# Attention and feed-forward layer: rewritten instruction orders at the opening, step 4, the change of phase and the end

## The chip, the cores and the metric

The kernel runs on one core of a Trainium2 chip. The metric is the device time of one execution in microseconds. Engines: PE (TensorE), DVE (VectorE), ACT (ScalarE), POOL (GpSimd) and SP (SyncE), which here only issues DMAs. They run side by side and meet at semaphores.

## The reference

x has 8 x 1024 x 512 elements, float32. Two blocks, each with a residual and a layernorm:

```python
q = (x @ Wq.T + bq).reshape(B, S, H, D)      # k, v likewise; q, k = rope(q), rope(k); H 16, D 32
qk = einsum('bshd,bstd->bsht', q, k) / sqrt(D)
att = softmax(qk, axis=-1)                   # over the 16 heads of one position
out = einsum('bsht,bstd->bshd', att, v)
out = swapaxes(out, 1, 2).reshape(B, S, E)
x = layernorm(x + out @ Wo.T + bo)
g = einsum('th,ih->ti', x, gate_w) * gate_s  # gate, up, down: ternary, 1408 wide
u = einsum('th,ih->ti', x, up_w) * up_s
x = layernorm(x + einsum('ti,hi->th', silu(g) * u, down_w) * down_s)
```

## The kernel before

**Precision.** Operands are split into a high and a low part, and a product takes hi x hi, hi x lo and lo x hi: `project` (L594 to L604) runs 12 matmuls of 128 x 512 for one tile and one weight.

**Phase 1, attention.** 64 tiles of 128 rows make 32 units (UNITS) of two tiles, t = 0 and 1. A unit m runs through a pipeline over five steps: split_x and low_x (high and low part of x), project_qk and project_v (PE), add_bias, sines (DVE), rotate (POOL, two instructions: cosine and add), turn_k and turn_q (DVE transposes), spread_k (ACT, four copies), score (PE, 128 small matmuls), subtract_top (DVE), exponent (ACT), sums_of_prob, scale_prob, turn_prob (DVE), spread_p (ACT, four copies), weigh_values (PE, 128 small matmuls, which needs v8, loaded again from DRAM by load_v after store_v), high_of_heads (ACT), low_of_heads (DVE), project_heads (PE, the output projection, row t of each unit), add_residual, aggregate (DVE), rstd_of (POOL), shift_of (DVE), normalise_x1 (ACT), turn_x1 (DVE), store_x1. Step s does unit s - 1's projections and score, unit s - 2's softmax and weigh_values, unit s - 3's heads and unit s - 4's layernorm. Every engine has its own written order. Steps 0 to 3 are written out for each engine (on SP and, before, for step 3 on DVE, through `step`), step 4 is called once with a number (OPENING = 4), steps 5 to 31 are a hardware loop, step 32 is called once more.

**Slabs.** Beside it the feed-forward weights are prepared, one of 32 slabs a step: ffn_slabs(s) (L414 to L427, SP) stores slab s - 2's parts (four DMAs, after f_lo_done) and loads slab s - 1 (13 DMAs in the trace); sums_of_slab (POOL, four instructions), high_of_slab (ACT), low_of_slab (POOL), top_of_slab (ACT).

**Between the phases.** `lo_top` shows whether any weight has a low part. DVE reduces it, PE joins it (L710), DVE sets the flag (L1681), SP and PE read it and branch, here to the exact variant (with_lo False).

**Phase 2.** The feed-forward network over 8 groups (SUPERS) of 8 tiles, 11 chunks (NJ) j each, with seven products P1 to P7 a chunk, sums on DVE, copies and silu on ACT, down1 and down2 (the down projection, rows r = 0 to 3 of 128 into four banks each). In group 0 the last units' attention is finished between the chunks (rest_of_attention). At the end of a group, read_row scales a bank, add_rows (POOL) or add_row (DVE) adds x1 (`xr`), stats_of, moments, shifts, normalise; in the last group down2's row 3 of the last two chunks runs after all else (rest_of_down2, L804).

## Time and profile before

| | |
|---|---|
| time, median of 3 | 1778.35 us |
| the profiled execution | 1778.3 us, span 1776.5 us |
| PE busy | 1716.8 us (97%), 15138 matmuls |
| PE weight loads | 1406.2 us (79%) |
| DVE busy | 1383.4 us (78%) |
| ACT busy | 942.1 us (53%) |
| POOL busy | 812.9 us (46%) |
| chain that ended last | PE 91%, issue 2%, DVE 2%, SP queue 2%, POOL 1% |

The span runs from the first to the last instruction. In rows of a timeline "idle before" is how long the engine had stood before the instruction, with what released it; "issue" stands for time in which it waited for nothing that the profile shows.

### The profile page before, as it was taken

What the parts mean: (1) busy time and instruction counts of PE and PEld (TensorE: products, weight loads), DVE (VectorE), ACT (ScalarE), POOL (GpSimd) and SP (SyncE); (2) the same over time, 40 slices, a digit from 0 to 9 for tenths busy, and PEclk for the clock granted to TensorE, in tenths of its full rate; (3) what the DMA queues carried; (4) which work ended last, traced back from release to release, by engine and by line L of the source; (5) the groups of instructions that cost most, each with busy time, mean ns of one, the idle gap of its engine ahead of it and who ended that gap; (6) DMA issues with size and microseconds to landing.
All of it is one profiled execution on the core that took longest, in us unless ns stands there. A gap on an engine that the chain in (4) does not pass through costs nothing.

```text
span 1776.5 us, 40766 instructions
## 1 busy us (share of the span) xinstructions
PE 1716.8 (97%) x15138; PEld 1406.2 (79%) x15138; DVE 1383.4 (78%) x1980; ACT 942.1 (53%) x1457; POOL 812.9 (46%) x697
## 2 busy tenths in 40 slices
PE   7889999999999999999799999999999999999997
PEld 5767888888888888888578888888888888888885
DVE  7878999998999999998756766677676776767756
ACT  4545556545655555465535455554555545555453
POOL 5778888888888888887300110201102011020112
PEclk9989999999999999999899999999999999999999
DMA  6585776787677767868674452644526445254341
GB/s 190 104 171 142 164 178 165 153 179 176 159 153 177 173 161 163 179 166 195 186 243 134 134 165 84 206 151 133 171 81 202 151 134 170 90 194 151 96 165 71
DMA packets 447191, 278.06 MB, mean 157 GB/s; under 512 B 261408, under 2 KB 385696, under 8 KB 447136
## 3 DMA queue, kind: packets, MB, share of 16 engines
q1 hardware_dynamic: 447136, 277.37, 58.5%
q8 instruction: 30, 0.49, 0.1%
q14 instruction: 25, 0.20, 0.0%
HBM read 183.97 MB, written 93.32 MB: 156 GB/s over the span
## 4 chain that ended last, share of the span: by engine, by line
PE 91%; issue 2%; DVE 2%; SPq 2%; POOL 1%; DMA 1%; ACT 1%; POOLq 0%; ACTq 0%; DVEq 0%
PE ps_x L599 13%; PE ps_x L603 12%; PE ps_x L600 12%; PE ps_s L755 9%; PE ps_s L760 8%; PE ps_x L755 7%; PE ps_x L760 7%; PE ps_x L766 4%; PE ps_x L770 4%; PE ps_s L671 3%; PE ps_a L633 2%; PE ps_s L766 2%; PE ps_a L766 2%; PE ps_a L770 2%; PE ps_s L770 2%
## 5 line engine op out<-in xcount | busy, mean ns | idle before, releaser
L599 PE MATMUL ps_x<-wqkv_hi,xc_hi 128*128 128x512 f32 x768 | 305.6, 398 | 18.6 <-POOL xc_lo L1127 8.0
L603 PE MATMUL ps_x<-wqkv_hi,xc_lo 128*128 128x512 f32 x768 | 301.6, 393 | 0.0
L600 PE MATMUL ps_x<-wqkv_lo,xc_hi 128*128 128x512 f32 x768 | 301.6, 393 | 0.0
L1261 POOL TENSOR_TENSOR z<-z,xr 128x512 f32<-128x512 f32 x62 | 79.7, 1310 | 483.9 <-DVE z L1575 483.9
L755 PE MATMUL ps_s<-x_hi,slot 128*128 128x512 f32 x672 | 264.9, 394 | 3.1 <-DVE hid L1508 2.1
L760 PE MATMUL ps_s<-x_lo,slot 128*128 128x512 f32 x672 | 262.2, 390 | 0.0
L901 ACT ACTIVATE kX<-kT 32x512 f32<-32x512 f32 x256 | 160.8, 628 | 168.8 <-DVE kT L1346 166.5
L1149 POOL TENSOR_TENSOR qk_cos<-qk_in,rot 128x512 f32<-128x512 f32 x128 | 204.1, 1594 | 79.7 <-DVE qk_in L1323 58.2
L755 PE MATMUL ps_x<-x_hi,slot 128*128 128x512 f32 x560 | 220.0, 393 | 7.4 <-ACT x_hi L1058 4.8
L760 PE MATMUL ps_x<-x_lo,slot 128*128 128x512 f32 x560 | 218.9, 391 | 0.0
L1155 POOL TENSOR_TENSOR qk_cos<-qk_cos,qk_sin 128x512 f32<-128x512 f32 x128 | 203.9, 1593 | 10.7 <-DVE qk_sin L1330 0.7
L599 PEld LDWEIGHTS ps_x<-wqkv_hi,xc_hi 128*128 128x128 f32 x768 | 145.7, 190 | 53.6 <-issue 11.7
L603 PEld LDWEIGHTS ps_x<-wqkv_hi,xc_lo 128*128 128x128 f32 x768 | 145.7, 190 | 31.1
L600 PEld LDWEIGHTS ps_x<-wqkv_lo,xc_hi 128*128 128x128 f32 x768 | 146.0, 190 | 29.7
L1508 DVE TENSOR_TENSOR hid<-ps_s,hid 128x512 f32<-128x512 f32 x88 | 60.7, 690 | 129.0 <-ACT hid L1010 129.0
L755 PEld LDWEIGHTS ps_s<-x_hi,slot 128*128 128x128 f32 x672 | 126.4, 188 | 38.2 <-ACT u L1039 4.9
L1255 POOL TENSOR_TENSOR rs<-mv,pw 128x4 f32<-128x4 f32 x16 | 22.5, 1405 | 273.0 <-DVE mv L1595 273.0
L760 PEld LDWEIGHTS ps_s<-x_lo,slot 128*128 128x128 f32 x672 | 126.5, 188 | 25.3
L766 PE MATMUL ps_x<-wd,h 128*128 128x512 f32 x352 | 137.0, 389 | 0.0
L770 PE MATMUL ps_x<-wd,h 128*128 128x512 f32 x352 | 137.0, 389 | 0.0
L755 PEld LDWEIGHTS ps_x<-x_hi,slot 128*128 128x128 f32 x560 | 105.8, 189 | 32.7 <-issue 7.9
L760 PEld LDWEIGHTS ps_x<-x_lo,slot 128*128 128x128 f32 x560 | 105.7, 189 | 21.7
(116 smaller groups left out, 3730.9 us busy)
## 6 DMA issues: line engine op xcount, KB each, us to landing
slot<-gu_hi SPq DMA_DIRECT2D x88, 896.0 KB, 5.0
xc<-x_cols SPq DMA_DIRECT2D x32, 512.0 KB, 5.5
v_rows<-v_in SPq DMA_DIRECT2D x32, 512.0 KB, 4.3
v<-v_rows SPq DMA_DIRECT2D x32, 512.0 KB, 5.2
res<-x_rows SPq DMA_DIRECT2D x64, 256.0 KB, 3.6
x_rows<-x_out SPq DMA_DIRECT2D x32, 512.0 KB, 2.8
x_cols<-x_turn SPq DMA_DIRECT2D x128, 128.0 KB, 2.6
wide<-x_cols SPq DMA_DIRECT2D x64, 256.0 KB, 5.1
```

Of the source, the lines that this page charges most:

```text
L599: pe.matmul(out, hi[:, k], w_hi[w][:, k], start=(k == 0), stop=False)
L600: pe.matmul(out, hi[:, k], w_lo[w][:, k], start=False, stop=False)
L603: last = pe.matmul(out, lo[:, k], w_hi[w][:, k], start=False, stop=(k == KE - 1))
L755: pe.matmul(out[:, :], slot[:, WEIGHTS[i], cols], x_hi[:, i, k], start=start, stop=False, skip_group_check=True)
L760: last = pe.matmul(out[:, :], slot[:, WEIGHTS[i], cols], x_lo[:, i, k], start=False, stop=stop, skip_group_check=True)
L766: pe.matmul(out[:, :], h_hi[h][:, rows], wd[:, j], start=first, stop=False, skip_group_check=True)
L770: return pe.matmul(out[:, :], h_lo[h][:, rows], wd[:, j], start=False, stop=last, skip_group_check=True)
L901: last = act.activation(kX[32 * c:32 * c + 32, t, :, c], kT[32 * c:32 * c + 32], ACT.Copy)
L1149: pool.tensor_tensor(qk_cos[:, w].rearrange("p (h d) -> p h d", h=H), qk_in[:, w].rearrange("p (h d) -> p h d", h=H), table_of(m)[:, t, 0] ...
L1155: pool.tensor_tensor(qk_cos[:, w], qk_cos[:, w], qk_sin[:, w], ALU.add).then_inc(rotated[w], 1)
L1261: pool.tensor_tensor(z[:, h, r], z[:, h, r], xr[:, r], ALU.add).then_inc(z_added[h], 1)
L1508: dve.tensor_tensor(hid2[:, j], bank_y[:, :], hid2[:, j], ALU.add).then_inc(c22_done, 1)
```

## The change

Orders of the same instructions are rewritten; no arithmetic is added or removed.

- **Opening.** SP's steps 0 to 3, PE's, ACT's, POOL's and DVE's orders are new: PE runs qk(1) whole before score(0), qk(2,0) before score(1), and weigh_values(1) between the two rows of heads(0). On SP, load_v(1) is now written behind ffn_slabs(2), and load_rope(2) waits only for unit 0's rotations.
- **Step 4.** On SP ffn_slabs comes after store_x1; on ACT the slab's high part after spread_k(m, 0); on POOL the slab's sums after rotate(m, 0, 0) and its low part after rotate(m, 1, 1). On PE, in steps 4 and 32, weigh_values stands between heads' rows.
- **Change of phase.** POOL does the last slab after the first sums of x. ACT mixes high_of_x with what is left of attention. DVE does row 0 of add_residual(29) in step 32, and low_of_x(P1), low_of_heads(30), row 1 after it; subtract_top(31) comes after the flag.
- **First chunks.** sums_of_prob(31) and scale_prob(31) in j = 0, turn_prob(31) and spread_p(31) in j = 1, each one chunk sooner.
- **End.** For the last group, chunks 7 to 10 of down2 run row by row (by_rows); x1's last rows are loaded at j = 6 into `raw`; DVE's statistics are earlier.

The diff, cut to its core ("..." for what is left out):

```diff
@@ -386,7 +389,7 @@
...
-            at_least(sp, rotated[w], 2 * m)
+            at_least(sp, rotated[w], 2 if m == 2 else 2 * m)
...
@@ -435,28 +438,38 @@
...
+        late = isinstance(s, int) and s == OPENING
...
-        if (m := unit_of(s, 0, UNITS)) is not None and m > 1:
+        if (m := unit_of(s, 0, UNITS)) is not None:
...
-        if (m := unit_of(s, 2, UNITS)) is not None:
-            load_v(m)
-        if s > 2:
+        load_v(s - 2)
+        if not late:
...
-        if (m := unit_of(s, 4, UNITS)) is not None:
-            store_x1(m)
-        if (m := unit_of(s, 0, UNITS)) is not None and m > 1:
+        store_x1(s - 4)
+        if late:
+            ffn_slabs(s)
+        if (m := unit_of(s, 0, UNITS)) is not None:
...
-        if (m := unit_of(s, 4, UNITS)) is not None:
-            store_x1_cols(m)
-        if (m := unit_of(s, 2, UNITS)) is not None:
-            load_residual(m)
-        if (m := unit_of(s, 1, UNITS)) is not None:
-            store_v(m)
-        if s == 1 or s == 2:
-            ffn_slabs(s)
-
-    for s in range(UNITS + 1):
+        store_x1_cols(s - 4)
+        load_residual(s - 2)
+        store_v(s - 1)
+
+    store_v(0)
+    load_x(2)
+    ffn_slabs(1)
+    load_v(0)
+    load_rope(2)
+    load_residual(0)
+    store_v(1)
+    load_x(3)
+    ffn_slabs(2)
+    load_v(1)
+    load_rope(3)
+    ffn_slabs(3)
+    load_residual(1)
+    store_v(2)
+    for s in range(OPENING, UNITS + 1):
...
@@ -471,13 +484,16 @@
...
-        if h == 0:
+        if is_last(n) and h == 1:
+            sp.wait_ge(blo_done, OPS * SUPERS)
+            sp.wait_ge(z_added[1], ROWS * n)
+        elif h == 0:
...
-        sp.dma_start(xr[:, :, :], x1_supers[n, h]).then_inc(xr_loaded[h], 16)
+        sp.dma_start(rows_of_x1(n, h)[:, :, :], x1_supers[n, h]).then_inc(xr_loaded[h], 16)
...
@@ -505,7 +521,7 @@
...
             store(last, 1)
-        if j == NJ and is_last(n):
+        if j == 6 and is_last(n):
             load_rows(n, 1)
...
@@ -609,10 +625,10 @@
...
-    def project_heads(s, m):
+    def project_heads(s, m, rows=(0, 1)):
         pe.wait_ge(ahi_done, 2 * m + 2)
         pe.wait_ge(alo_done, 2 * m + 2)
-        for t in range(2):
+        for t in rows:
             if (now := unit_of(s, 1, UNITS)) is not None:
...
@@ -679,10 +699,13 @@
...
             project_v(m)
+        straight = isinstance(s, int)
         if (m := unit_of(s, 3, UNITS)) is not None:
-            project_heads(s, m)
+            project_heads(s, m, (0,) if straight else (0, 1))
         if (m := unit_of(s, 2, UNITS)) is not None:
             weigh_values(m)
+        if straight and (m := unit_of(s, 3, UNITS)) is not None:
+            project_heads(s, m, (1,))
         if (m := unit_of(s, 1, UNITS)) is not None:
...
@@ -690,18 +713,18 @@
     project_qk(0, 1)
     project_v(0)
     project_qk(1, 0)
+    project_qk(1, 1)
     score(0)
-    project_qk(1, 1)
     project_v(1)
+    project_qk(2, 0)
     score(1)
-    project_qk(2, 0)
+    project_qk(2, 1)
     weigh_values(0)
-    project_qk(2, 1)
     project_v(2)
-    project_heads(3, 0)
+    project_heads(3, 0, (0,))
     weigh_values(1)
+    project_heads(3, 0, (1,))
     score(2)
-
     unit_steps(pe, step, LAGS, UNITS, 1)
     project_heads(UNITS + 1, UNITS - 2)
@@ -801,6 +824,14 @@
...
+        def by_rows(n):
+            for r, chunks in ((0, (7, 8, 9)), (1, (7,)), (0, (10,)), (1, (8, 9, 10)), (2, (7, 8, 9, 10)),
+                              (3, (7, 8, 9, 10))):
+                for j in chunks:
+                    if r == 0:
+                        inputs_of_down2(n, j)
+                    down2(n, j, (r,))
+
         def rest_of_down2(n):
...
@@ -854,7 +885,7 @@
...
-            for j in range(1, NJ - 2):
+            for j in range(1, 7 if is_last(n) and not with_lo else NJ - 2):
...
@@ -950,16 +981,21 @@
...
-        ending = isinstance(s, int) and s == UNITS
-        slabs(s)
+        late, ending = (isinstance(s, int) and s == n for n in (OPENING, UNITS))
+        if not late:
+            slabs(s)
...
+        if late:
+            top_of_slab(s - 3)
...
+        if late:
+            high_of_slab(s - 2)
...
@@ -1070,21 +1104,22 @@
             return
         first = isinstance(n, int) and n == 0
         if first:
+            high_of_x(0, P1)
             high_of_heads(UNITS - 2)
+            high_of_x(0, P2)
+            high_of_slab(UNITS - 1)
+            high_of_x(0, P5)
             top_of_slab(UNITS - 1)
-            high_of_x(0, P1)
-            high_of_x(0, P2)
+            high_of_x(0, P6)
+            high_of_x(0, P7)
             exponent(UNITS - 1)
             act.wait_ge(power_set, 3)
             act.activation(table[:, :], ones[:, :], ACT.Silu)
-            high_of_x(0, P5)
             act.wait_ge(scale_loaded, 16)
         for j in range(NJ + 1):
             if j > 0:
                 copy_u3(n, j - 1)
             if first and j == 0:
-                high_of_x(0, P6)
-                high_of_x(0, P7)
                 copy_s1(0, 0)
                 high_of_x(0, P4)
                 copy_u2(0, 0)
@@ -1194,41 +1229,41 @@
...
+            if late:
+                sums_of_slab(s - 2)
...
+            if late:
+                low_of_slab(s - 2)
...
-        if ending:
-            sums_of_slab(UNITS - 1)
...
-        if ending:
-            low_of_slab(UNITS - 1)
-        elif (m := unit_of(s, 1, UNITS)) is not None:
+        if (m := unit_of(s, 1, UNITS)) is not None and not ending:
...
-    for t in range(2):
-        rotate(1, t, 1)
-        rotate(1, t, 0)
+    rotate(1, 0, 1)
+    rotate(1, 0, 0)
+    rotate(1, 1, 1)
...
+    rotate(1, 1, 0)
...
+    rotate(2, 0, 1)
...
+    rotate(2, 0, 0)
...
-    rotate(2, 0, 1)
+    rotate(2, 1, 1)
...
-    rotate(2, 0, 0)
-    sums_of_slab(1)
-    rotate(2, 1, 1)
-    low_of_slab(1)
...
-    add_output_bias(0, 1)
...
-    sums_of_slab(2)
+    sums_of_slab(1)
+    low_of_slab(1)
+    add_output_bias(0, 1)
...
@@ -1241,6 +1276,8 @@
...
     first_sums_of_x()
+    sums_of_slab(UNITS - 1)
+    low_of_slab(UNITS - 1)
     for m in range(UNITS - 3, UNITS):
...
@@ -1450,6 +1487,10 @@
...
             add_bias(m, 0, 2)
+        if isinstance(s, int) and s == UNITS:
+            add_bias(UNITS - 1, 1, 2)
+            add_residual(UNITS - 3, (0,))
+            return
         if (m := now3) is not None:
...
@@ -1463,43 +1504,58 @@
     add_bias(0, 0, 0)
     sines(0, 0, 0)
     add_bias(0, 1, 1)
+    low_x(1, 0)
+    add_bias(0, 0, 2)
     turn_k(0, 0)
-    low_x(1, 0)
     sines(0, 1, 1)
-    add_bias(0, 0, 2)
+    add_bias(0, 1, 2)
+    low_x(1, 1)
     add_bias(0, 1, 0)
-    add_bias(0, 1, 2)
     sines(0, 1, 0)
     turn_k(0, 1)
     turn_q(0, 0)
-    low_x(1, 1)
     add_bias(1, 0, 1)
     sines(1, 0, 1)
     turn_q(0, 1)
     add_bias(1, 0, 0)
     sines(1, 0, 0)
-    subtract_top(0)
     add_bias(1, 1, 1)
     turn_k(1, 0)
     sines(1, 1, 1)
-    sums_of_prob(0)
+    subtract_top(0)
+    add_bias(1, 0, 2)
     add_bias(1, 1, 0)
     turn_q(1, 0)
     sines(1, 1, 0)
+    sums_of_prob(0)
+    add_bias(1, 1, 2)
+    turn_k(1, 1)
     scale_prob(0)
-    turn_k(1, 1)
+    turn_q(1, 1)
+    add_bias(2, 0, 1)
+    sines(2, 0, 1)
     turn_prob(0)
-    turn_q(1, 1)
-    add_bias(1, 0, 2)
-    add_bias(1, 1, 2)
+    add_bias(2, 0, 0)
+    sines(2, 0, 0)
+    subtract_top(1)
+    turn_k(2, 0)
+    add_bias(2, 1, 1)
+    sums_of_prob(1)
+    sines(2, 1, 1)
+    turn_q(2, 0)
+    low_of_heads(0)
+    add_bias(2, 1, 0)
     low_of_weight(W_ORDER[3])
-    step(3)
+    scale_prob(1)
+    sines(2, 1, 0)
+    turn_prob(1)
+    turn_k(2, 1)
+    turn_q(2, 1)
+    add_bias(2, 0, 2)
+    add_bias(2, 1, 2)
+    add_residual(0)
+    aggregate(0)
     unit_steps(dve, step, LAGS, UNITS, 1)
-
-    low_of_heads(UNITS - 2)
-    subtract_top(UNITS - 1)
-    dve.wait_ge(lo_seen, SLABS)
-    dve.tensor_reduce(lo_top1[:, :], lo_top[:, :], AX.X, ALU.max).then_inc(lo_reduced, 1)
     def sum_c22(n, j):
         c = NJ * n + j
@@ -1641,7 +1697,6 @@
...
             shift_of(UNITS - 3)
-        if j == 1:
             sums_of_prob(UNITS - 1)
...
@@ -1676,14 +1729,20 @@
         first = isinstance(n, int) and n == 0
         if first:
             low_of_x(0, P1)
+            low_of_heads(UNITS - 2)
+            add_residual(UNITS - 3, (1,))
+            aggregate(UNITS - 3)
             low_of_x(0, P2)
+            low_of_x(0, P5)
+            dve.wait_ge(lo_seen, SLABS)
+            dve.tensor_reduce(lo_top1[:, :], lo_top[:, :], AX.X, ALU.max).then_inc(lo_reduced, 1)
+            sum_t(0, 2)
             dve.wait_ge(lo_joined, 1)
             dve.tensor_scalar(inexact[0:1, :], ps_x[0][0:1, 0:1], 0.0, None, ALU.is_gt).then_inc(flag_set, 1)
-            low_of_x(0, P5)
-            sum_t(0, 2)
-            sum_t(0, 3)
+            subtract_top(UNITS - 1)
             low_of_x(0, P6)
             low_of_x(0, P7)
+            sum_t(0, 3)
         for j in range(NJ + 1):
             if j > 0:
                 sum_c22(n, j - 1)
@@ -1711,15 +1770,24 @@
...
-                if j >= 8:
-                    stats_of(n, 0, j - 8)
+                if j == 8:
+                    stats_of(n, 0, 0)
+                    stats_of(n, 0, 1)
+                if j == 9:
+                    stats_of(n, 0, 2)
+                    stats_of(n, 0, 3)
...
-            stats_of(n, 0, 3)
...
-        for r in range(3):
-            read_row(n, 1, r)
-        if is_last(n):
+            read_row(n, 1, 0)
...
+            read_row(n, 1, 1)
+            stats_of(n, 1, 0)
+            read_row(n, 1, 2)
+            stats_of(n, 1, 1)
+            add_row(n, 2)
+        else:
+            for r in range(3):
+                read_row(n, 1, r)
...
```

## Rows read from the trace of the kernel before

**Rows 1.** Busy us by stretch (stretch, width, PE, PEld, DVE, ACT, POOL, clock, DMA, GB/s).

```profile
18.00:75.30 57.30, 51.58 (x569) 41.57 (x568) 55.12 (x65) 26.54 (x42) 40.58 (x29) 0.94 0.39 99
8.05:86.80 78.75, 70.96 (x881) 57.20 (x881) 66.46 (x82) 39.26 (x62) 58.38 (x47) 0.96 0.54 142
86.80:122.09 35.29, 27.54 (x354) 22.32 (x353) 25.14 (x37) 15.74 (x25) 26.62 (x27) 0.90 0.75 167
122.09:150.76 28.67, 27.32 (x352) 22.33 (x353) 23.65 (x33) 14.14 (x22) 21.09 (x19) 0.94 0.59 135
793.70:818.90 25.20, 25.20 (x353) 20.87 (x352) 23.20 (x32) 13.78 (x23) 21.39 (x20) 1.00 0.79 162
818.90:861.80 42.90, 33.19 (x382) 27.05 (x379) 34.58 (x44) 21.66 (x32) 30.85 (x23) 0.90 0.86 209
861.80:920.00 58.20, 52.66 (x329) 39.64 (x330) 38.00 (x61) 27.92 (x46) 4.39 (x7) 0.96 0.63 202
```

**Rows 2.** Timeline of PE, opening (start, length, instruction, idle before it and releaser).

```profile
30.78 0.77 PE L599 MATMUL ps_x<-wqkv_hi,xc_hi 128*128 128x512 f32 x1 [2.83 <-DVE v_in L1323]
...
54.62 1.91 PE L671 MATMUL ps_s<-kX,qT 128*16 128x64 f32 x64 [2.48 <-ACT kX L901]
...
81.18 1.48 PE L633 MATMUL ps_a<-pX,v 64*32 64x64 f32 x128 [0.27 <-ACT pX L941]
...
109.10 0.77 PE L599 MATMUL ps_x<-wo_hi,aT_hi 128*128 128x512 f32 x1 [5.75 <-DVE aT_lo L1386]
...
121.63 0.31 PE L671 MATMUL ps_s<-kX,qT 128*16 128x64 f32 x4 [1.87 <-issue]
```

**Rows 3.** Timeline of POOL, opening.

```profile
26.52 1.29 POOL L1155 TENSOR_TENSOR qk_cos<-qk_cos,qk_sin 128x512 f32<-128x512 f32 x1
...
60.30 1.92 POOL L1169 TENSOR_TENSOR f_lo<-f_all,f_hi 128x792 fp32r<-128x792 f32 x1 [0.98 <-ACT f_hi L914]
```

**Rows 4.** Timeline of DVE, opening.

```profile
26.71 1.65 DVE L1293 TENSOR_TENSOR xc_lo<-xc,xc_hi 128x512 fp32r<-128x512 f32 x1
...
74.04 1.29 DVE L1377 STREAM_TRANSPOSE pT<-prob 128x512 f32<-128x512 f32 x2
```

**Rows 5.** Timeline of the SP queue, opening.

```profile
62.25 0.33 SPq L418 DMA_DIRECT2D dn_hi<-f_hi  x1
...
64.31 9.04 SPq L426 DMA_DIRECT2D f_all<-ffn_w  x13
...
73.94 0.41 SPq L396 DMA_DIRECT2D v<-v_rows  x1
```

**Rows 6.** Transfers issued from 70 to 80 us, KB each, us to landing.

```profile
v<-v_rows SPq DMA_DIRECT2D x1, 512.0 KB, 6.9
```

**Rows 7.** Timeline of ACT, opening.

```profile
78.58 2.55 ACT L941 ACTIVATE pX<-pT,own 128x512 f32<-128x512 f32 x4
...
94.68 0.87 ACT L914 ACTIVATE f_hi<-f_all 128x792 fp32r<-128x792 f32 x1 [10.12 <-POOL f_all L1183]
```

**Rows 8.** Timeline of PE, change of phase.

```profile
849.43 0.77 PE L599 MATMUL ps_x<-wo_hi,aT_hi 128*128 128x512 f32 x1 [2.96 <-issue]
...
861.80 0.76 PE L755 MATMUL ps_x<-x_hi,slot 128*128 128x512 f32 x1 [4.78 <-ACT x_hi L1058]
```

**Rows 9.** Timeline of POOL, change of phase.

```profile
843.01 0.37 POOL L1178 TENSOR_TENSOR f_all<-f_all 128x88 f32<-128x88 f32 x1 [5.42 <-DMA f_all<-ffn_w]
```

**Rows 10.** Timeline of DVE, change of phase.

```profile
845.80 0.69 DVE L1408 TENSOR_TENSOR y<-ps_x,res 128x512 f32<-128x512 f32 x1 [4.38 <-POOL res L1143]
...
857.07 0.15 DVE L1681 TENSOR_SCALAR inexact<-ps_x 1x1 int32<-1x1 f32 x1 [2.51 <-PE ps_x L710]
```

**Rows 11.** Timeline of PE, its last instruction.

```profile
1763.63 0.39 PE L770 MATMUL ps_s<-wd,h 128*128 128x512 f32 x1
```

**Rows 12.** Timeline of DVE, end.

```profile
1765.91 0.67 DVE L1575 TENSOR_TENSOR z<-ps_s,dscale 128x512 f32<-128x512 f32 x1
...
1769.20 0.38 DVE L1593 BATCH_NORM_AGGREGATE mv<-st 128x2 f32<-128x6 f32 x4
```

44 lines of the change are left out of this document (23 added, 21 removed).

## The prediction

> **What bounds the kernel now.** I read the page first: TensorE (PE) is busy 97% of the span, so the time is PE's work plus the places where PE waits. The table by stretch shows them. In a steady step of the attention loop PE is busy all of 25.20 us and VectorE (DVE) 23.20 of it: nothing there can be won by an order, and the loop body is not changed. The opening is not like that: from PE's first matmul to the end of score(2) PE is busy 70.96 of 78.75 us, step 4 takes 35.29 and step 5 takes 28.67, against 25.20 steady. The change of phase (818.9 to 861.8) leaves PE 9.7 us idle, the next 58.20 us leave 5.5 [rows 1]. PE's last matmul ends at 1764.0, so 12.5 us of the 1776.5 us span are a tail without PE [rows 11]. What any order could still win is thus some 20 us in the opening, 10 to 15 around the change of phase and a few in the tail: about 40 us, 2% of the time. The timelines say who holds PE up. In the opening: 2.83 us for v_in, 2.48 us for kX, 5.75 us for aT_lo at 109.1, 1.87 us with nothing in the profile to wait for ("issue") [rows 2]. Behind aT_lo stands ScalarE (ACT): f_hi of slab 2 waited 10.12 us for POOL and held the heads and the exponent behind it [rows 7]. At the change of phase: 2.96 us before heads(30), called issue, but DVE's add_residual stood before the low part of these heads and waited 4.38 us for the residual, and this for POOL, blocked 5.42 us on a slab's DMA; then 4.78 us between the flag and the first product [rows 8 to 10].
>
> [...]
>
> **Part A, to the end of score(2), before at 86.8.** No instruction is added or removed; all is order. (1) v(0)'s biases come before turn_k(0,0) and before sines: biased[2] is there when v(0) ends at 27.8, so the 2.83 us stall and its clock go: -4.3 us. (2) PE now runs both halves of qk(1) before score(0), and v(1) is over at about 46. qk(2,0) needs xc_lo of unit 2. ACT must first do exponent(0), which waits for subtract_top(0), which DVE reaches only after turn_k(1,0): walked through with the durations of the trace, split_x(2,0) ends at 46.9 and POOL's low_x at 48.2. A new stall of 2.2 us, 0 to 4, and 1.4 of clock. (3) The 2.48 us for kX goes, since score(1) follows qk(2,0): -2.5 and its clock, -1. After this PE is at weigh_values(1) at about 74 instead of 81.2 (2.7 us of this because only row 0 of heads(0) stands before it). (4) But what weigh_values(1) waits for does not come sooner. Its probabilities: DVE is busy 55.12 of the 57.30 us from 18 to 75.3, where turn_prob(1) ended, and the new order has the same instructions before turn_prob(1), so at most 2.2 us can go; with spread_p's 2.55 us behind it that is 76 to 79 [rows 1, 4, 7]. Its v8: the SP queue gives it out behind ffn_slabs(2), which waits for f_lo of slab 0 and then takes from 62.25 to 73.35, 11.1 us, and the load took 6.9 us to land [rows 5, 6]. In the new order low_of_slab(0) is behind one rotation more on POOL (rotate(2,0,0), two instructions of 1.3 us or more), and unit 0's turn_prob is later on DVE: I get f_lo at 64.9 instead of 62.2 [rows 3]. So v8 is issued at 76.0 and lands between 79.5 (if slabs take 9 us and the load as little as 5) and 82.9; I take 81.2. (5) From there PE does weigh_values(1), row 1 of heads(0), which it had behind it before, and score(2): 1.4 + 2.7 + 1.9, with the small steps between them and 1.5 of clock after 7 us idle, 89.0. Part A: +2.2 us (-2 to +5). All is won in (1) to (3) and waited away in (4).
>
> [...] DVE's xc_lo took 1.65 us at 26.71, since POOL's add ran from 26.52 to 27.81; the same instruction takes 0.6 when POOL is idle [rows 3, 4]. [...]
>
> **Part B, step 4, before 35.29.** ACT's high_of_heads(1) and exponent(2) no longer stand behind high_of_slab(2), which before could start only at 94.68, its sums waiting for the slab [rows 7]. So DVE runs as in a steady step, the 5.75 us and the clock behind it go. The order heads row 0, weigh_values, heads row 1 brings PE to weigh_values(2) 2.7 us sooner than steady, and spread_p(2), now behind high_of_slab's 0.87 us, is 0.9 us late. The 1.87 us of issue stay: 25.2 + 0.9 + 1.9 + 1.3 of clock = 29.3, -6.0 us (-8 to -3).
>
> **Part C, step 5, before 28.67.** What was moved comes back here. low_of_slab(2) now follows rotate(3,1,1): behind three rotations, about 19 us after score(2). The SP queue gives out slab 3's loads behind it: +11.1 us of issue, +2 to land, 32 us after score(2). Step 5 begins 29.3 after it. POOL's sums_of_slab(3) stands before rstd_of and rotate(4,0,1), and ACT's step 5 begins with high_of_slab(3), as step 4's did: exponent(3) comes about 4 us later than in a steady step, DVE's slack is 2.0 us of 25.20 [rows 1], so heads(2) waits 1.5 to 3.5 us. I take 2.2, no new clock beyond the 1.7 there was, less 0.7: +1.5 us (-2 to +5). Opening in all: -2.3 us (-9 to +6).
>
> **Part D, change of phase.** In step 32 DVE no longer waits for row 1's residual before low_of_heads(30); POOL does the residual before the slab and the first sums before it. By the walk: score(31) ends at 846.9 (issue stall kept), aT_lo is ready at 846.1, so the 2.96 us go. heads(30) end at 852.5. DVE's flag follows x_lo of P2 and P5 and sum_t: 853 to 854.3 instead of 857.07. Flag to first product stays 4.7 us (857.1 to 861.8): first product at 858.3 instead of 861.8, -3.5 us (-5 to 0, where the SP queue's wait for the slab stores, unchanged at about 856, holds slots 1 and 2). A gain above 5 would need the 4.7 us to shrink.
>
> **Part E, first chunks.** sums_of_prob and scale_prob (1.2 + 0.6 + 1.2 us) now stand on DVE before sum_c22(0,0): up to 1.9 us of new stall; spread_p (2.55 us on ACT) in chunk 1 delays copy_u3(1). In return turn_prob no longer holds up high_of_hid1(1). The stalls of this stretch are 5.5 us before [rows 1]; I cost this at 0 (-3 to +3).
>
> **Part F, end.** by_rows does the same matmuls, but rows 0, 1 and 2 finish 22, 16 and 8 matmuls (5.0, 3.6 and 1.8 us) before the last. DVE now reads, adds and measures rows 0 to 2 meanwhile. Before, it read row 3 at 1765.91, 1.9 us after PE's end, and came to the moments at 1769.20 [rows 12]. Now row 3 is read at 1764.7; add, two bn_stats: moments at 1767.5. h2(10)'s low part stands behind two more bn_stats, 0.3 us of PE. -1.7 us (-3 to 0). The rows of x1 loaded early into raw hide behind PE.
>
> **Sum.** -2.3 - 3.5 + 0 - 1.7 = -7.5 us, from the profiled execution's 1778.3 (span 1776.5, 1.8 around it), which is the median of the runs shown (1778.35) to 0.05: 1770.8 us.
>
> **Rivals.** R1, the walk above: stalls move more than they vanish, 1771, own range 1765 to 1776: 0.5. R2, the slab loads do not bind: v8 is there at 78 and slab 3 before step 5 needs it. [...] Against it: v8 landed at 80.8 in the trace. Part A -1, B -6, C -2, D -4, F -2: 1763: 0.27. R3, slower: slab loads bind harder. Place: ffn_slabs(2) and (4) before load_v(1) and sums_of_slab(3). Each microsecond that f_lo(0) comes later than 64.9 moves weigh_values(1), and with it all behind; a late slab 3 holds exponent(3) as slab 2 did before (10.12 us [rows 7]). If A is +8 and C +6, the opening is +8, less 5.2 of D and F: 1781. It decides from an opening of +5.3 on: 0.13. R4, gains of the two ends are eaten by E and only the stalls' places change: 1776 to 1778: 0.1.
>
> The range takes in R1, most of R2 and the near part of R3: 1759 to 1781. A measurement of this kernel can tell 2%, 36 us, from no change; all idle time that orders touch is about that. Faster by over 2%: 0.01, within 2%: 0.98, slower: 0.01.
>
> **What would show it.** A: no idle at 28; weigh_values(1) on PE near 82, released by v8's DMA, after 6 to 9 us idle; score(2) ending at 88 to 90. B: no wait for aT_lo above 1 us. C: ACT's f_hi waiting for POOL f_all at the start of step 5. D: first product at 858 to 859. F: tail of 11 instead of 12.5 us. If weigh_values(1) starts before 79, or exponent(3) is on time, R2 holds; if score(2) ends after 92, R3.

## The result

The changed kernel takes 1774.89 us (median of 16 runs, 1771.93 to 1777.96), the kernel before 1778.68 beside it: a ratio of 0.998, 95% interval 0.9972 to 0.9987, so 2 to 5 us less. The forecast was 7.5 us less. Single executions can fall in a slower state (one of the kernel before took 3898.40 us), and the ratios leave those out. The profiled executions differ by 3.1 us (span 1776.5 and 1773.4). First the stretches of after that answer to [rows 1]: to the end of score(2), step 4, step 5, change of phase, first chunks (columns as there).

```profile
8.05:90.77 82.72, 71.80 (x881) 57.37 (x881) 66.84 (x86) 40.07 (x63) 58.26 (x48) 0.92 0.52 137
90.77:120.80 30.03, 26.42 (x352) 20.92 (x352) 24.64 (x32) 13.28 (x22) 21.90 (x19) 1.00 0.59 128
120.80:149.18 28.38, 25.95 (x355) 21.18 (x353) 25.36 (x33) 15.87 (x25) 25.00 (x26) 1.00 0.77 184
817.25:858.91 41.66, 31.49 (x383) 25.54 (x379) 37.62 (x45) 22.02 (x32) 32.19 (x23) 0.92 0.90 215
858.91:917.10 58.19, 50.85 (x322) 38.03 (x323) 35.94 (x58) 27.96 (x45) 4.39 (x7) 0.97 0.60 194
```

Put beside before, with where each stretch begins, the 3.1 us come together like this:

| Stretch | before | after | difference | forecast |
|---|---|---|---|---|
| PE's start to the end of score(2) (A) | to 86.80 | to 90.77 | +4.0 | +2.2 |
| step 4 (B) | 35.29 | 30.03 | -5.3 | -6.0 |
| step 5 (C) | 28.67 | 28.38 | -0.3 | +1.5 |
| loop, 150.76 to 818.90, 149.18 to 817.25 | 668.14 | 668.07 | -0.1 | 0 |
| change of phase, to the first product (D) | 42.90 | 41.66 | -1.2 | -3.5 |
| first product to 895.05, 893.49 (E) | 33.25 | 34.58 | +1.3 | 0 |
| from there to the end of the span (F) | 881.45 | 879.91 | -1.5 | -1.7 |

The timeline of PE in the changed kernel shows the stalls behind these numbers, in the opening and at the change of phase; [rows 2, 8] are the ones they replace.

```profile
49.90 0.47 PE L615 MATMUL ps_x<-wqkv_hi,xc_hi 128*128 128x512 f32 x1 [2.95 <-POOL xc_lo L1162]
...
79.58 1.80 PE L649 MATMUL ps_a<-pX,v 64*32 64x64 f32 x108 [4.90 <-issue]
83.43 0.64 PE L649 MATMUL ps_a<-pX,v 64*32 64x64 f32 x20 [2.06 <-issue]
...
138.93 0.47 PE L615 MATMUL ps_x<-wo_hi,aT_hi 128*128 128x512 f32 x1 [1.38 <-issue]
...
844.36 0.47 PE L615 MATMUL ps_x<-wo_hi,aT_hi 128*128 128x512 f32 x1 [0.78 <-issue]
...
858.91 0.77 PE L778 MATMUL ps_x<-x_hi,slot 128*128 128x512 f32 x1 [8.75 <-issue]
...
871.25 0.47 PE L778 MATMUL ps_s<-x_hi,slot 128*128 128x512 f32 x1 [1.95 <-DVE hid L1564]
878.89 0.50 PE L778 MATMUL ps_s<-x_hi,slot 128*128 128x512 f32 x1 [1.44 <-ACT hid L1044]
```

The stalls for v_in and kX are gone, as is the one of 5.75 us for aT_lo. In their place stand one for unit 2's xc_lo and two at weigh_values(1). The 2.96 us before heads(30) are down to 0.78, and the first product waits 8.75 instead of 4.78 us. From the start of weigh_values(1) to the end of score(2), PE's granted clock was at its lower level most of the time (0.50 to 87.9 and 1.00 after it, 0.63 on average; a 128x512 matmul started every 0.43 us at 0.50 and every 0.23 at 1.00; columns as in [rows 1]):

```profile
79.58:90.77 11.19, 9.13 (x269) 7.38 (x269) 1.67 (x5) 5.08 (x8) 3.38 (x4) 0.63 0.39 90
```

On the other queues of the changed kernel, first SP's:

```profile
67.01 6.93 SPq L429 DMA_DIRECT2D f_all<-ffn_w  x13
74.04 0.38 SPq L399 DMA_DIRECT2D v<-v_rows  x1
...
850.95 0.38 SPq L399 DMA_DIRECT2D v<-v_rows  x1
```

POOL's and ACT's timelines at the start of step 5:

```profile
122.25 0.37 POOL L1213 TENSOR_TENSOR f_all<-f_all 128x88 f32<-128x88 f32 x1 [6.23 <-DMA f_all<-ffn_w]
```

```profile
123.91 0.87 ACT L945 ACTIVATE f_hi<-f_all 128x792 fp32r<-128x792 f32 x1 [8.82 <-POOL f_all L1218]
```

DVE's: the flag, and the end (row 3 read, its moments), beside [rows 10, 12].

```profile
850.67 0.14 DVE L1741 TENSOR_SCALAR inexact<-ps_x 1x1 int32<-1x1 f32 x1
...
1763.37 0.69 DVE L1631 TENSOR_TENSOR z<-ps_s,dscale 128x512 f32<-128x512 f32 x1
...
1766.08 0.38 DVE L1649 BATCH_NORM_AGGREGATE mv<-st 128x2 f32<-128x6 f32 x4
```

So the flag is 6.4 us sooner and the first product 2.9. What PE does between them is the branch: its own instruction, seen by its line (duration in ns, then its start), before and then changed:

```profile
L874 PEldq COMPARE_BRANCH  x1: 3524/3524/3524, 858.1 to 858.1; - x1
```

```profile
L905 PEldq COMPARE_BRANCH  x1: 6413/6413/6413, 852.3 to 852.3; - x1
```

The branch takes 2.9 us longer. The load of the flag ahead of it takes 1.09 instead of 0.48 us, and the first product starts 0.17 us after the branch ends in both; together these are the 3.5 us between 4.7 and 8.2. The transfers tell what the branch lacked. A queue "instruction" (q8) moved 30 blocks of 16 KB in this execution (30 packets, 0.49 MB). They are read here as PE's program, since the branch ends 1.5 us after such a block has landed, and the stalls of PE in its straight code told of below end 1.2 to 1.5 us after one. The transfers view, changed kernel, 850.7 to 855.5 and then 855.5 to 857.5 (packets, MB, share of 16 engines):

```profile
q1 hardware_dynamic: 5343, 1.12, 136.3%
issues: line engine op xcount, KB each, median us to landing
v<-v_rows SPq DMA_DIRECT2D x1, 512.0 KB, 6.3
...
q1 hardware_dynamic: 577, 0.07, 41.7%
q8 instruction: 1, 0.02, 4.7%
```

In the kernel before, 857.1 to 859.1 hold no packet at all, and 859.1 to 861 this one, 2.2 us after the flag (and one of 8 KB on another queue):

```profile
q8 instruction: 1, 0.02, 2.9%
```

In the changed kernel it comes 5.1 us after the flag, when the last unit's v8 load (4096 pieces of 128 bytes) has nearly gone through. In both the branch ends 1.5 us after the block has landed.

### The profile page after: what moved, and what is told of

It reads as the page before. It is cut to its first block, busy times and chain, and to the rows that moved or that the text cites. A ratio compares the mean times of both kernels' runs of the same rounds, so it can differ in the third digit from the quotient of the medians.

```text
span 1773.4 us, 40772 instructions
## 1 busy us (share of the span) xinstructions
PE 1713.4 (97%) x15138; PEld 1402.5 (79%) x15138; DVE 1384.7 (78%) x1980; ACT 942.7 (53%) x1457; POOL 813.9 (46%) x697
## 4 chain that ended last, share of the span: by engine, by line
PE 89%; DVE 3%; issue 3%; ACT 1%; POOL 1%; DMA 1%; SPq 1%; POOLq 0%; ACTq 0%; DVEq 0%
PE ps_x L615 12%; PE ps_x L619 12%; PE ps_x L616 12%; PE ps_s L778 8%; PE ps_s L783 8%; PE ps_x L778 7%; PE ps_x L783 7%; PE ps_x L789 4%; PE ps_x L793 4%; PE ps_s L691 3%; PE ps_a L649 2%; PE ps_a L793 2%; PE ps_a L789 2%; PE ps_s L789 2%; PE ps_s L793 2%
```

## The experiments

Each ran beside the kernel before on the same chip; ratios are against it, with their 95% interval. The kernel before had medians of 1778.3 to 1778.8 us beside them. An interval is 3 to 5 us wide, so two variants less than about 3 us apart are not told apart by their times, and what is said of them rests on one trace each. Such traces vary too: four kernels with the changed kernel's orders up to step 6 (changed, late v8 load, softmax back, v8 read twice) begin step 5 at 120.9 to 121.4 and step 6 at 149.2 to 150.5, and two with both heads first begin step 5 at 116.7 and 119.7, step 6 at 147.4 and 148.2. First three edits alone on the changed kernel, and the end alone on the kernel before.

**The late v8 load.** load_v(UNITS - 1) leaves its place ahead of the branch and is issued behind the slot loads of chunk 0.

```
             ffn_slabs(UNITS + 1)
-            load_v(UNITS - 1)
...
+                if isinstance(n, int) and n == 0 and j == 0:
+                    load_v(UNITS - 1)
```

> The changed kernel, with the load of v8 for unit 31 issued after the branch (behind the first slot loads) instead of before it. Theory: after the flag PE needs one block of its program through the DMA rings, and in the changed kernel the block stood behind the 128-byte packets of this load (block landed 5 to 6.5 us after the flag, against 2 to 3 before the change). Then the first product comes 4.7 us after the flag instead of 8.2, near 855.5 instead of 858.9, and the time falls by 3 us (2 to 3.5) against the changed kernel. Rival: the block is held by the slab stores issued at the same time, or by nothing on the rings: then the gap stays at 8 us and the time is the same within 0.5 us.

Measured: 1772.34 us, 0.9965 (0.9951 to 0.9979), span 1770.5. Flag at 851.30, PE's block 2.4 us behind it, first product 5.16 behind it. The timeline of PE in this kernel:

```profile
856.46 0.76 PE L779 MATMUL ps_x<-x_hi,slot 128*128 128x512 f32 x1 [5.67 <-DVE x_lo L1618]
```

The view names x_lo as the last releaser, but the branch (3.67 us) ended 0.17 us before the product here as well. The slab stores were in flight as in the changed kernel (the last landed 3.3 us after the flag), so the rival that they hold the block is out: the v8 load in flight is what held the first product.

**Both rows of heads(0) ahead of weigh_values(1).**

```
-            project_heads(3, 0, (0,))
+            project_heads(3, 0)
             weigh_values(1)
-            project_heads(3, 0, (1,))
```

> The changed kernel, with both rows of heads(0) before weigh_values(1) in the opening, as before the change. Theory: weigh_values(1) waits for v8, not for PE's order, so it starts at 79.6 as in the changed kernel, the 4.9 us wait shrinks to about 2.2, and score(2) ends 2.7 us sooner plus up to 2.4 us of the clock that row 1 lost: 86 to 88 instead of 90.8, time 3 to 5 us less than the changed kernel. Rival: the wait is one of the program block's arrival on PE, which comes a fixed time after it is asked for: then the whole shifts by the 2.7 us and the time does not fall.

Measured: 1773.98 us, 0.9977 (0.9968 to 0.9987), span 1771.1. The 4.90 us shrink to 2.74, row 1 no longer runs at the clock's lower level (1.00 to 79.6, a matmul every 0.23 us and not every 0.43), and step 5 begins at 116.7 instead of 120.9. But there heads(2) wait longer than in the changed kernel (1.38), and of 4.2 us 1.7 are left at step 6. The gain of 3 to 5 us that was expected is not there: 0.9 us by the medians, which the intervals don't tell from nothing, and 2.3 by the spans. PE, this kernel:

```profile
136.36 0.47 PE L615 MATMUL ps_x<-wo_hi,aT_hi 128*128 128x512 f32 x1 [3.02 <-issue]
```

**The last unit's softmax in its old chunks.** sums_of_prob and scale_prob again under j == 1, turn_prob and spread_p again under j == 2.

```
                     shift_of(UNITS - 3)
+                if j == 1:
                     sums_of_prob(UNITS - 1)
...
-                        if first and j == 1:
+                        if first and j == 2:
                             turn_prob(UNITS - 1)
```

> The changed kernel, with the last unit's softmax sums, scaling, turning and spreading back in chunks 1 and 2 as before the change. Theory: these moves cost 1.3 us (from the first product to 893 the changed kernel lost 1.3 us more than before): the stall of 1.95 us for hid at 871 goes, a stall of 1.8 us for u near 880 comes back, and the time is 0.5 to 1.5 us less than the changed kernel. Rival: the loss came from elsewhere (the clock after the longer gap), and the time is the same or 0.5 us more.

Measured: 1772.67 us, 0.9967 (0.9955 to 0.998), span 1771.3. The first product is at 858.91 as in the changed kernel, and PE's stalls behind it are the kernel before's to 0.01 us; the point at 893.49 moves to 891.90. In this trace the softmax one chunk sooner costs 1.6 us, just over what was expected.

```profile
881.43 0.50 PE L778 MATMUL ps_x<-x_hi,slot 128*128 128x512 f32 x1 [1.83 <-ACT u L1073]
886.50 0.50 PE L778 MATMUL ps_s<-x_hi,slot 128*128 128x512 f32 x1 [0.94 <-DVE hid L1564]
891.90 0.50 PE L778 MATMUL ps_s<-x_hi,slot 128*128 128x512 f32 x1 [0.75 <-ACT u L1073]
```

**The end alone,** on the kernel before (by_rows in the last super, rows_of_x1, row reads and statistics; nothing of the attention).

```
-                    else:
+                    elif not is_last(n):
...
-                    add_row(last, 2)
-                    stats_of(last, 1, 0)
                     read_row(last, 1, 3)
```

> The kernel before with only the end changed: down2's last four chunks row by row, x1's last rows loaded early, statistics earlier. Theory: 2.0 us less than before (the tail behind PE 10.1 instead of 12.5 us, PE's own end 0.4 us later), all else at its old place. Rival: part of that is noise between two executions, and it is 1 us or less.

Measured: 1777.55 us, 0.9995 (0.9985 to 1.0004), span 1776.8. Behind the end of PE's last matmul (1766.31 + 0.39) 10.1 us are left instead of 12.5 [rows 11], as in the changed kernel; this execution was 2.3 us slower ahead of it, at the change of phase (5.14 instead of 2.96 us before heads(30), which the edit does not touch). The 2.4 us in the tail are seen, in the whole time the noise hides them.

**The three together.**

> The changed kernel with three edits at once, each of which was run alone: the last unit's v8 load issued behind the phase branch (alone -2.55 us in the medians, -2.9 in the span), both rows of heads(0) ahead of weigh_values(1) (alone -0.9 and -2.3), the last unit's softmax sums, turning and spreading back in their old chunks (alone -2.2 and -2.1). Theory T: the three lie in different stretches and each takes away a wait of its own, so they add: span 1773.4 - 2.9 - 2.3 - 2.1 = 1766.1, or, by the medians, 1774.9 - 5.7 = 1769.2; first product 2.3 us earlier than with the late load alone (856.46), at about 854.2. Rival: something else sets the start of the chunks, above all the slot loads or the stored rows of P2 and P5, and then the sooner flag is waited away again: the first product stays at about 856.5 and the median at 1770.5 to 1772.

Measured: 1770.33 us, 0.9954 (0.994 to 0.9967), span 1767.2. First product at 854.97, 5.4 us behind the flag. By the spans 6.2 of 7.3 us are there, but the profiled execution is the fastest of the five; by the medians 4.6 of 5.7. What is missing is in the opening (step 6 at 148.22; 147.44 with both heads first alone).

**A double dose:** v8 of the last unit read a second time, into DRAM, right behind the first (changed kernel).

```
             load_v(UNITS - 1)
+            sp.dma_start(twice[:, :].rearrange("p (t b d) -> p t b d", t=2, b=C * B4),
+                         v_in2[UNITS - 1]).then_inc(twice_stored, 16)
```

> The changed kernel with the last unit's v8 read a second time behind the first, into DRAM that nothing reads: 4096 more pieces of 128 bytes just before the flag. T1: PE's program block for the first chunk waits behind these pieces, which take some 5 us a load; the block, 5.1 us after the flag in the changed kernel, comes 8 to 10 us after it, the first product 10 to 12 us after the flag (8.24 in the changed kernel) and the time is 2 to 5 us longer: 1777 to 1780. Rival R: the delay comes from the slab stores alone, which are as they were: flag to first product stays within 1 us of 8.24 and the time within 1 us of 1774.9.

Measured: 1775.47 us, 0.9983 (0.9973 to 0.9993). The block comes 4.0 us after the flag (851.85), with both copies under way, and the product 7.1 after it. The 10 to 12 us expected from flag to product did not come: twice the traffic delays nothing more, and the block does not wait until the pieces queued ahead of it are through (v8 itself landed at 858.93, the block started at 855.81). The transfers from 855.7 to 858, with the block and the second copy at once:

```profile
q1 hardware_dynamic: 2812, 0.36, 147.8%
q8 instruction: 1, 0.02, 3.8%
issues: line engine op xcount, KB each, median us to landing
twice<-v_rows SPq DMA_DIRECT2D x1, 512.0 KB, 8.9
```

**load_v(1) ahead of ffn_slabs(2),** on the changed kernel.

```
             load_x(3)
+            load_v(1)
             ffn_slabs(2)
-            load_v(1)
```

> The changed kernel with load_v(1) ahead of ffn_slabs(2) in the SP queue, so that v8 of unit 1 is issued when weigh_values(0) has ended (about 66.4) instead of at 74.04. T1: v8 is no longer what weigh_values(1) waits for; spread_p(1), which ends at 78.25, is: weigh_values(1) starts at 78.3 instead of 79.58, and since its 4.9 us of idle only shrink to 3.6, the half-speed stretch behind it stays: end of score(2) at 89 to 90, the whole -1 to -1.5 us at the end of step 4. Rival: v8 was the whole of the stall and PE goes on at 76 or before: then spread_p(1) would have to be sooner, and the gain would be 4 us and more. Second rival: slab 2, issued up to 2 us later, holds step 4's high_of_slab: the gain is given back, 0.

Measured: 1775.72 us, 0.9982 (0.9971 to 0.9992). v8 is issued at 65.48; weigh_values(1) starts at 78.59, released by spread_p, and the 2.06 us inside it are gone. Step 4 begins at 86.90, 3.8 us sooner, where 1 to 1.5 were expected; step 5 at 115.24, 5.7 us sooner than in the changed kernel; step 6 begins at 150.46, 1.3 later and within the 149.2 to 150.5 of the kernels named above. The timelines of PE, ACT and POOL in this kernel:

```profile
136.70 0.77 PE L615 MATMUL ps_x<-wo_hi,aT_hi 128*128 128x512 f32 x1 [4.84 <-issue]
```

```profile
122.14 0.87 ACT L945 ACTIVATE f_hi<-f_all 128x792 fp32r<-128x792 f32 x1 [11.39 <-POOL f_all L1218]
```

```profile
120.04 0.37 POOL L1213 TENSOR_TENSOR f_all<-f_all 128x88 f32<-128x88 f32 x1 [6.59 <-DMA f_all<-ffn_w]
```

PE came 5.7 us sooner and slab 3 only 2.2 (120.04 for 122.25): the whole lead is paid back.

**low_of_slab(2) one rotation sooner,** on the kernel with the three edits.

```
                         sums_of_slab(s - 2)
+                        low_of_slab(s - 2)
                     rotate(m, 1, 1)
-                    if late:
-                        low_of_slab(s - 2)
```

> The kernel with the three edits, and in step 4 POOL's low_of_slab(2) one rotation sooner (ahead of rotate(3,1,1)), so that the SP queue gives out slab 3 about 2.6 us sooner. T (part C of the prediction: slab 3's landing holds f_hi, exponent(3) and with them heads(2) in step 5): with both rows of heads first, POOL waited 5.27 us for slab 3 until 119.71 and PE's heads(2) had 3.02 us of idle at 136.36; with slab 3 2.6 us sooner this falls to 1 us or less, step 6 starts 2 us sooner and the time is 1 to 2 us less than with the three edits alone. Rival: what is late for heads(2) is not the slab but DVE's own row of work (turns of k and q): the 3.02 us stay within 0.5 and the time too; rotate(3,1,1), now 1.9 us later, could even cost 1 us.

Measured: 1769.42 us, 0.9942 (0.9929 to 0.9956), span 1765.9. SP's slab 3 is issued at 108.61 instead of 110.01, POOL waits 3.05 instead of 6.61 us for it, step 6 begins at 146.31 instead of 148.22. But 1.8 of these 1.9 us were there at the start of step 5 already (117.86 for 119.66), 0.4 even at the start of step 4, ahead of the edit; heads(2) wait 1.03 instead of 1.39. So this run alone does not show that the sooner slab is what moved step 6, and by the medians (0.9 us) the two kernels are not told apart.

**The load at the flag, on the kernel before.**

```
             ffn_slabs(UNITS + 1)
+            sp.wait_ge(flag_set, 1)
             load_v(UNITS - 1)
```

> The kernel before, with the last unit's v8 load made to wait for the flag (there it is issued at 851.57, long before the flag at 857.07), so that it runs in the 5 us behind the flag as it does in the changed kernel. If a v8 load in flight is enough to hold up PE's program block: the block, 2.2 us after the flag in the kernel before, comes 4 to 5 us after it, the first product 7 to 8.2 us after the flag instead of 4.73, and the time is 2 to 4 us longer. If the changed kernel's 8.24 us come from something else in its order (slab stores close to the flag, DVE's or ACT's new order): flag to first product stays at 4.7 to 5.2 and the time within 1 us.

Measured: 1779.24 us, 1.0004 (0.9995 to 1.0013). Flag at 854.90, block 3.2 us behind it, product 6.2 behind it: 1.0 and 1.5 us later than in the kernel before, where 1.8 and 2.3 at the least were expected. In flight alone the load costs less than half of the 3.5 us that the changed kernel lost from flag to product. The time does not show it, since this execution's flag came 2.2 us sooner (0.98 instead of 2.96 us before heads(30)).

**Step 5 in step 4's order,** with load_v(1) first, on the changed kernel.

```
-                late = isinstance(s, int) and s == OPENING
+                late = isinstance(s, int) and s in (OPENING, OPENING + 1)
...
```

That is SP's line; ACT's and POOL's are changed alike, and POOL's sums of slab 3 leave the end of step 4.

> The changed kernel with load_v(1) ahead of ffn_slabs(2), and step 5 in the order that the change gives to step 4 (ACT's high_of_slab(3) behind the heads, the exponent and the first spread_k; POOL's sums and low part of slab 3 behind rotations; SP's slab transfers behind store_x1). With load_v(1) first alone, step 5 began at 115.1 instead of 120.8, and all of it was waited away again at heads(2), 4.84 us, and behind it: step 6 began at 150.4. Theory S (slab 3, which lands at about 120 whatever PE does, holds POOL's queue and ACT's): without it in front, heads(2) is on time (under 1 us of idle), step 5 takes 25.5 to 27 us, step 6 begins at 141 to 143 and the time is 6 to 8 us less than with load_v(1) alone, about 1768. Rival: the debt only moves one step further, to slab 4 in step 6, and half or more of it is waited away there: 1771 to 1774. Second rival: heads(2) wait for something else, and nothing moves.

Measured: 1776.32 us, 0.9988 (0.9978 to 0.9998). heads(2) wait 1.41 us, against 4.84 with load_v(1) first alone, though PE comes to them sooner (131.0 for 131.9): with slab 3 out of their way the heads are nearly on time. Step 5 takes 29.1 us, more than the 25.5 to 27 expected, and step 6 begins at 143.47, 5.7 us sooner than in the changed kernel; then POOL waits 6.24 us for slab 4 and heads(3) wait:

```profile
164.90 0.77 PE L615 MATMUL ps_x<-wo_hi,aT_hi 128*128 128x512 f32 x1 [4.80 <-issue]
```

Step 7 begins at 175.67, 0.8 later than in the changed kernel. The rival held in its mechanism: the debt moved to the next slab. In the time even less is won than by the rival's 1771 to 1774.

**All of these together.**

> The three edits (late v8 load of the last unit, heads(0) whole first, softmax sums in the old chunks), low_of_slab(2) one rotation sooner, and the two edits of the run above (load_v(1) ahead of ffn_slabs(2), step 5 in step 4's order). Theory S: the opening gains what it gained above, 6 to 8 us less than the 4 to 5 that the edits to the opening share: about 2 to 4 us below the 1769.4 of the kernel without the last two edits, 1765.5 to 1767.5. Rival: they do not add, since PE ahead of DVE and POOL waits at another place in steps 4 to 6: 1768.5 to 1770.

Measured: 1770.55 us over all seven executions (1769.87 without one of 1882.70, the only one with a trace, of which no line is used), 0.9949 (0.9935 to 0.9963). The rival's time: they do not add. Where PE waits instead was not seen.

**Slab 2's work one rotation sooner,** on the kernel with the three edits.

```
+                    if late:
+                        sums_of_slab(s - 2)
                     rotate(m, 0, 0)
                     if late:
-                        sums_of_slab(s - 2)
+                        low_of_slab(s - 2)
                     rotate(m, 1, 1)
```

and on ACT high_of_slab(2) ahead of spread_k(3, 0).

> The kernel with the three edits, and in step 4 the whole of slab 2's work one rotation sooner (POOL: sums ahead of rotate(3,0,0), low part behind it; ACT: high_of_slab(2) ahead of the first spread_k), so that SP gives out slab 3's loads 3 to 5 us sooner (at 103.5 to 105.5; 108.61 with the low part one rotation sooner, 110.01 without). Theory S (the chain f_lo of one slab, 7 to 9 us of issue, landing, sums, high, low of the next sets when the loop is in step): slab 3 is there at the start of step 5, heads(2) on time, step 6 begins at 144 to 146 and the time is 1768 to 1769.5, 0 to 1 us below the variant with the low part one rotation sooner (1769.4), since PE's own start of step 5 (117 to 119) now binds. Rival: POOL's rotations of unit 3 come 1.9 to 3.4 us later and hold score(3): 1770 to 1772.

Measured: 1766.24 us, 0.9935 (0.9922 to 0.9949), span 1764.5; 1.8 us better than the best expected, though not by the way expected. heads(2) no longer stall and step 6 begins at 145.99, but slab 3 is issued at 107.68 and not at 103.5 to 105.5, and step 7 begins at 171.67, only 0.3 us sooner than with the low part one rotation sooner. Of the 1.4 us between the two spans 1.0 come after the first product, where PE's granted clock is at its lower level for 3.0 us here (to 855.5) and for 5.6 there (to 858.5). So in these two traces it is where the low stretch fell, not the slab; the 3.2 us between the two medians the runs do not explain.

**The same with load_v(1) first.**

> The same with load_v(1) ahead of ffn_slabs(2). Alone, that brought PE 5.7 us sooner to step 5 and won nothing, since slab 3 landed at 120 all the same. Theory S: with slab 3 4 to 6 us sooner as well, the two fit together: step 5 begins at 113 to 115, heads(2) wait less than 1.5 us, step 6 begins at 140 to 142.5, and the time is 3 to 5 us below the kernel with the three edits (1770.3): 1765.5 to 1767.5. Rival (the debt moves on, as it did to slab 4 in step 6): heads(3) wait 3 us or more in step 6, and step 7 begins at 171 or later, as in the variants before: 1769 to 1770.5.

Measured: 1764.95 us, 0.9931 (0.9918 to 0.9945), span 1762.8: by the medians 9.9 us under the changed kernel (8.7 by the ratios), and the lowest, though its interval overlaps the last one's. Step 5 begins later than expected (116.9), since heads(1) wait 3.21 us in step 4, and step 6 at 143.65 and not by 142.5. But nothing is paid back behind it: heads(2) and heads(3) have no stall, and step 7 begins at 169.35, 5.5 us sooner than in the changed kernel. POOL in this kernel waits for slab 3 only this long:

```profile
113.89 0.37 POOL L1213 TENSOR_TENSOR f_all<-f_all 128x88 f32<-128x88 f32 x1 [1.35 <-DMA f_all<-ffn_w]
```

One table for the opening, start of each step on PE and of slab 3's work on POOL (us):

| Kernel | step 4 | slab 3 | step 5 | step 6 | step 7 |
|---|---|---|---|---|---|
| before | 86.7 | 115.2 | 122.1 | 150.8 | 176.5 |
| changed | 90.7 | 122.3 | 120.9 | 149.2 | 174.9 |
| load_v(1) first | 86.9 | 120.0 | 115.2 | 150.5 | 176.2 |
| and step 5 late | 85.8 | 128.7 | 114.4 | 143.5 | 175.7 |
| both heads first | 87.9 | 119.7 | 116.7 | 147.4 | 173.2 |
| three edits | 88.4 | 120.9 | 119.7 | 148.2 | 173.9 |
| three, low sooner | 88.0 | 118.5 | 117.9 | 146.3 | 172.0 |
| three, slab 2 sooner | 88.4 | 118.2 | 119.0 | 146.0 | 171.7 |
| and load_v(1) first | 85.1 | 113.9 | 116.9 | 143.7 | 169.4 |

And one for the flag (us):

| Kernel | v8 of unit 31 | flag | block after flag | product after flag |
|---|---|---|---|---|
| end alone | through | 858.62 | 2.0 | 5.1 |
| before | through | 857.07 | 2.2 | 4.7 |
| late load | behind | 851.30 | 2.4 | 5.2 |
| three, low sooner | behind | 847.69 | 2.3 | 5.2 |
| three, slab 2 sooner | behind | 847.25 | 2.6 | 5.3 |
| and load_v(1) first | behind | 845.37 | 2.6 | 5.1 |
| three edits | behind | 849.59 | 2.8 | 5.4 |
| before, load at flag | in flight | 854.90 | 3.2 | 6.2 |
| softmax back | in flight | 851.86 | 3.9 | 7.1 |
| v8 read twice | in flight | 851.85 | 4.0 | 7.1 |
| both heads first | in flight | 849.01 | 4.0 | 7.2 |
| load_v(1) first | in flight | 851.83 | 4.4 | 7.6 |
| and step 5 late | in flight | 851.05 | 4.7 | 7.8 |
| changed | in flight | 850.67 | 5.1 | 8.2 |

## Why the prediction was right in most places and wrong in size

The stalls of the walk came and went nearly where it said; the gain is about half of the forecast by the medians (3.8 us beside the kernel before) and less by the spans. C has the wrong sign, and E, put at nothing, costs. In the spans 4.4 of 7.5 us are missing: 2.3 in D, 1.3 in E, 0.7 in the opening, where A came out 1.8 and B 0.7 dearer and C 1.8 cheaper, and 0.2 in F.

**D, the step that failed most.** "Flag to first product stays 4.7 us." The walk up to it was good: 0.78 instead of 2.96 us before heads(30), and the flag 33.4 us after the start of the stretch, where the walk, told in the times of the kernel before, had 34.1 to 35.4 (853 to 854.3 less 818.9). From flag to product it was 8.24 us, 3.5 more; less the 1.2 us by which the flag beat the walk, that is the 2.3 us missing in D. That the product still fell in the window named as D's sign (858.91, for 858 to 859) is chance: 1.65 us that the opening had won hid part of the loss. The 4.7 us were taken for a constant of the branch. By the traces they are the time to a program block (start 2.2 us after the flag, 0.9 us to land) and the 1.7 us from its landing to the product, and in the kernel before the flag was so late that v8's last packet had gone out (at 856.9). A flag 6.4 us sooner falls into the load. Moving the load behind the branch gave back 2.9 us of span, 2.6 of median; in the fourteen traces read (second table) the block comes 2.0 to 2.8 us after the flag where no v8 load is in flight (seven), and 3.2 to 5.1 where one is (seven). Had the prediction asked what the 4.7 us were made of, it would have asked what else the DMA queues carry at 851.

**A, mis-sized by 1.8 us.** What was forecast is there: no idle at 28, a new stall for xc_lo (2.95; forecast 2.2), f_lo of slab 0 at 64.89 (64.9), v8 as the last releaser, a start of weigh_values(1) ahead of the 81.2 taken (79.58, since the 13 loads took 6.93 us to issue and not 9 or more, and v8 5.4 to land). The wait itself was 4.9 us and not 6 to 9. What failed is the term behind it: from the start of weigh_values(1) to the end of score(2) the sum had 7.8 us (81.2 to 89.0), and PE took 11.2. Of the 3.4 us, 2.06 are a second stall in weigh_values(1) that the sum did not have, and the rest is the clock, priced at 1.5 us: 0.63 over 11.19 us is 8.3 us at the lower level, of which the stall fills 2.06, so at half speed (0.50) it cost about 3.1. The sooner start gave 1.6 us back.

Over the whole part the granted clock shows 0.92 over 82.72 us, 13.2 us at the lower level, against 0.96 over 78.75, 6.3 us. The second stall is a program block: nothing in weigh_values is waited for behind its first matmul, a 16 KB block starts at 81.04, and PE goes on 1.4 us after it has landed, as the branch ends 1.5 us after its own. In the seven other kernels in which v8 is the last releaser the same stall (1.50 to 2.37 us) ends 1.2 to 1.4 us after the block. With load_v(1) first the block comes at 74.34 already, during the wait, and the stall is gone. Undoing the order of heads(0) alone, so that row 1 runs ahead of the idle time, brought step 4 forward 2.8 us. In the span's own terms: idle 10.9 instead of 7.8 us, busy 0.8 more.

**The clock's terms.** The sum has 1.4, 1, 1.5 and 1.3 us for the clock, and a like amount in the -4.3: one price for every long stall, the author's estimate. No run shows such a price. In the kernel before the lower level (0.50) lasted 3.4 us behind each of the stalls of 2.83, 2.48 and 1.87 us, and 6.8 us from within the 5.75 on, always with about 1.7 us lost where PE worked; the 1.7 us taken for step 5 are the one at 121.63. In the changed kernel it lasted 3.4 us behind the 2.95 for xc_lo and 10.2 us around the 4.90 and 2.06, and did not come behind the 1.38. With v8 read twice, and with load_v(1) first and step 5 late, stalls for xc_lo of 2.90 and 2.93 us had nothing behind them (1.00 from 49 to 60).

**B, right** (30.03 for 29.3; no wait for aT_lo over 1 us), though not in its terms: the 1.3 us of clock did not come (1.00), while PE was idle 3.6 us and busy 1.2 us more than in a steady step. **C, right in mechanism, too dear:** f_hi of slab 3 waited 8.82 us for POOL and POOL 6.23 for the slab, as forecast, but heads(2) lost 1.38 us instead of 2.2, and the clock no more at all (1.00 for 0.94). What A lost and C did not are one thing: with PE later in step 5, slab 3 is less late. load_v(1) first shows it the other way round, 5.7 us won by step 5 and all of it lost by step 6. In eight kernels (changed, late load, softmax back, v8 twice, both heads first, and the three edits without or with slab 2 or its low part sooner) step 6 begins 26.9 to 28.2 us after POOL starts on slab 3, wherever PE began step 5. So A and C may not be estimated apart, and the rival in which slab loads bind harder had the right limit with the wrong sign of the sum: it is a ceiling on the gain, not a loss. That v8 was the releaser of weigh_values(1) was true, and without it step 4 begins 3.8 us sooner, but by step 6 nothing is left of that unless the slab is moved too.

**E, mis-sized by 1.3 us.** The two effects costed against each other to 0 do not cancel. DVE's 3 us of sums and scaling ahead of the chunk's sums hold hid at 871.25 (1.95), and ACT's spread_p holds it at 878.89 (1.44); the 1.83 us for u that vanish are the only return. Undone, 1.6 us come back.

**F, right in sum, by two misses that cancel:** the tail is 10.1 us instead of 12.5, better than the 11 named. After the end of PE's last matmul (1763.3) row 3 is read at once and the moments begin 2.8 us later; forecast were 0.7 and 3.5 us (1764.7 and 1767.5 less 1764.0). But PE itself took 0.9 us more from 893.49 to its last matmul than before from 895.05, where 0.3 were counted. Together -1.5 for -1.7.

**Open.** It stays open why the block takes 5.1 us in the changed kernel and 3.2 with the same load in the kernel before. In the latter the slab stores had all landed before the flag (852.5, flag at 854.9); in the changed kernel the last lands 3.4 us behind it. With the late load they are in flight too (3.3 us behind it), and the block comes after 2.4: stores alone cost little (2.3 to 2.8 us in five kernels, 2.0 and 2.2 with neither in flight). So load and stores together are the worst, but how the queues share the DMA engines the runs don't tell. Nor is the flag's own time what counts: in the changed kernel, with the softmax back and with v8 read twice the flag is at 850.67, 851.86 and 851.85, and the block starts at 855.75, 855.75 and 855.81. Twice the pieces made it no longer.

## What to carry to other kernels

Before a flag ahead of a branch is moved sooner, list the transfers that will be in flight at its new time, and put a load like v8's (512 KB in pieces of 128 bytes) behind the branch if it is not needed soon: here the program block then came 2.4 us after the flag instead of 5.1. In a start-up phase find the chain with the longest period (here a slab: low part, issue, landing, sums, high part) and move that one: PE brought forward alone gives its lead back one or two steps later, and the sum of terms by stretch counts it as won. Where two effects of unlike engines are costed against each other to nothing, ask which one stands ahead of PE's next input. And read a step's start from more than one trace: here those of kernels with the same opening differed by up to 2.9 us.
